# A two-layer graph network on one core: where the work buffers start in on-chip memory, modulo 64 bytes

## The chip, the core and the metric

The kernel runs on one core of a Trainium2 chip. The metric is the device time of one execution in microseconds. Before the change it is 2314.32 us, the median of three runs (2314.19 to 2317.76).

## What is computed

There are 128 graphs of 128 nodes with 256 features, `x[128,128,256]`, and an integer matrix `adj[128,128,128]`. Two layers follow each other for every graph, and no graph touches another. All is fp32.

Layer 0 (called A in the kernel):

```
q, k, v = x@Wq.T+bq, x@Wk.T+bk, x@Wv.T+bv          # 8 heads of 32
p = softmax(where(adj == 0, -16384, q k^T))
z = v;  4 times:  z = 0.9 * p z + 0.1 * v
x1 = layernorm(x + z) * gamma + beta
```

Layer 1 (called B, its feed-forward part C):

```
n = layernorm(x1)*g1+b1;  q, k, v = n@wq+bq, ...
p = softmax(q k^T / sqrt(32) + where(adj > 0, 0.1*adj*adj, -inf))
x2 = x1 + (p v)@wo + bo
out = x2 + gelu((layernorm(x2)*g2+b2)@w1 + b1) @ w2 + b2      # 256 -> 1024 -> 256
```

## The kernel before

Two graphs form a pair, and 64 pairs go through the kernel. The work on a pair is cut into some 80 small steps (a projection, a quarter of the softmax, one hop of `z`, ...). Their order is written out by hand in three lists: a head, one turn that repeats through the middle (each turn takes every step once, for pairs 0 to 5 turns back, so that up to six pairs are in work), and a tail. All engines walk through the same list, and each does its part of the steps; semaphores tie them together. PSUM is a ring of four banks (`ring_ps`) beside four more banks for the attention scores (`score_ps`).

TensorE does two sorts of matrix products:

- Products with weights run in the type float32r on operands that are split into a high and a low part, three matmuls for each product (high·high, high·low, low·high; `by_parts`, lines 374 to 378, and `down`, lines 507 to 517). Each has 256 moving columns and a stationary operand of 128 columns, which a weight load (LDWEIGHTS) of its own brings in. In the projections (`project`) and in `up` a work buffer moves (`inT_A`, `inT_B`, `inT_C`) and the weight is stationary. In `values`, `output` and `down` the weight moves and a work buffer is stationary (`inT_A`, `inT_B`, `oT`, `hT`).
- Scores, hops, and the transposes run on plain fp32. In a transposition the unit matrix `ident` moves and the work buffer is stationary; in scores and hops both operands are work buffers.

In the rows of the trace an operation is written out<-moving,stationary, and the digits at the end of buffer names are left out (`w_high` is `w1_high` on line 377 and `w2_high` on line 515).

The diff touches only the place of buffers in SBUF. `sb(name, shape)` (line 198) takes the next free bytes of every partition, in the order of the calls, and each buffer begins at a multiple of 32 bytes. Worked out from the shapes and this rule, the places are, as a remainder by 64 (by 128 in brackets):

| buffers | before | after |
|---|---|---|
| all weights of the float32r products (`wA`, `wB`, `wo`, `w1`, `w2`) | 0 (0) | 0 (0) |
| the bias, gamma and beta rows | 32 (32) | 32 (32) |
| `ident` | 32 (32) | 0 (64) |
| all work buffers from `x_sb` to `hT_low` | 0 (64) | 32 (32) |

Every slice that a matmul reads starts at a multiple of 512 bytes within its buffer (128 in the hops), so an operand has the remainder of its buffer. The order of the steps, the instructions, and the semaphores are not touched.

Of the kernel before, what the change touches and what calls it, by code (L numbers as in the profile page):

```python
# [13 lines left out]
P = 128  # L14
# [171 lines left out]
def build(nc, x, xT, adj, WqT, bq, WkT, bk, WvT, bv, gamma, beta, ln1_g, ln1_b, ln2_g, ln2_b,  # L186
# [10 lines left out]
    with ExitStack() as ctx:  # L197
        def sb(name, shape, dt=F32):
            return ctx.enter_context(nc.sbuf_tensor(name, shape, dt))
# [18 lines left out]
        bvA_row, bvB_row = sb("bvA_row", [P, H]), sb("bvB_row", [P, H])  # L218
        gamma_row, beta_row = sb("gamma_row", [P, H]), sb("beta_row", [P, H])
        bo_row, b2_row = sb("bo_row", [P, H]), sb("b2_row", [P, H])  # L220
        ident = sb("ident", [P, P])
        tenth, eps, minus_half = sb("tenth", [P, 1]), sb("eps", [P, 1]), sb("minus_half", [P, 1])


        sb("apart", [P, 16])
        x_sb = sb("x_sb", [P, GB, H])
        xT_sb = sb("xT_sb", [P, C, T])
        adj_sb = {l: sb(f"adj_{l}", [P, GB, P], I32) for l in "AB"}
# [702 lines left out]
```

## Time and profile before

| | us | share |
|---|---|---|
| median of three runs | 2314.32 | |
| the profiled execution | 2317.23 | |
| its span, first to last instruction | 2315.4 | |
| TensorE busy (PE) | 2266.6 | 98% |
| weight loads (PEld) | 2154.3 | 93% |
| ScalarE busy (ACT) | 1926.8 | 83% |
| VectorE busy (DVE) | 1749.9 | 76% |
| GpSimd busy (POOL) | 1520.4 | 66% |

PE's busy time is the union of its matmuls, which overlap each other: one of 276 ns may follow the one before it by 113. So the busy time tells that the engine always had work, not how fast it went; for that the start times in the order of time are to be read. Weight loads run beside the matmul before them.

### The profile page before, as it was taken

To read this page: it belongs to the slowest core of one execution; us is meant where nothing else is said; L and a number is where in the kernel's file an instruction comes from. 1 tells how busy PE (TensorE), PEld (TensorE's weight loads), DVE (VectorE), ACT (ScalarE), POOL (GpSimd) and SP (SyncE) were. 2 spreads that over 40 slices of the span, in tenths; PEclk is the share of its full clock that TensorE was granted. 3 is DMA by queue.
4 is the path that set the end of the run, shared out by engine and by line. 5 is a ranking of instruction groups with operands and counts; after the bars stand their busy time and mean duration, and the time that the engine had idled before them with its cause. 6 is when DMAs were issued, how large, how long until landed. Compare 5 with 4: busy or idle time off the path is not lost. (4 is left out here: it accounts for less than half of the span.)

```text
span 2315.4 us, 78263 instructions
## 1 busy us (share of the span) xinstructions
PE 2266.6 (98%) x29492; PEld 2154.3 (93%) x29492; DVE 1749.9 (76%) x6993; ACT 1926.8 (83%) x6478; POOL 1520.4 (66%) x1613
## 2 busy tenths in 40 slices
PE   5999999999999999999999999999999999999997
PEld 5899999999999999999999999999999999999987
DVE  3888777787787787787787787787787787778883
ACT  5788888898898898898898898898888888888874
POOL 4766666676666666667666666666666667676551
PEclk8999999999999999999999999999999999999998
DMA  4110101101101101101101101101101101101000
GB/s 124 32 29 22 39 25 34 38 25 34 39 25 34 38 23 36 38 20 39 39 20 38 38 20 39 38 21 38 39 20 39 38 20 38 38 21 43 16 15 15
DMA packets 95781, 76.88 MB, mean 33 GB/s; under 512 B 9648, under 2 KB 95152, under 8 KB 95408
## 3 DMA queue, kind: packets, MB, share of 16 engines
q1 hardware_dynamic: 94176, 71.73, 10.0%
q8 instruction: 239, 3.92, 0.7%
q14 instruction: 134, 1.10, 0.2%
q10 hardware_dynamic: 1232, 0.14, 0.0%
HBM read 55.06 MB, written 16.78 MB: 31 GB/s over the span
## 5 line engine op out<-in xcount | busy, mean ns | idle before, releaser
L580 ACT ACTIVATE probs<-probs,negmax 128x128 f32<-128x128 f32 x2048 | 797.0, 398 | 28.1 <-DVE negmax L704 22.0
L862 POOL TENSOR_TENSOR probs<-probs,rinv 128x512 f32<-128x512 f32 x512 | 534.3, 1064 | 138.7 <-DVE rinv L718 138.4
L580 ACT ACTIVATION_READ_ACCUMULATOR probs<-probs,negmax 128x1 f32 x2048 | 402.3, 196 | 0.0
L601 ACT ACTIVATE zT<-ring_ps 128x512 f32<-128x512 f32 x256 | 157.8, 617 | 182.4 <-PE ring_ps L459 182.2
L377 PE MATMUL ring_ps<-inT_C_high,w_high 128*128 128x256 f32 x1024 | 302.4, 295 | 5.3 <-DVE inT_C_low L675 4.0
L515 PE MATMUL ring_ps<-w_high,hT_high 128*128 128x256 f32 x1024 | 296.8, 290 | 1.0 <-DVE hT_low L790 1.0
L451 PE MATMUL ring_ps<-ident,probs 128*128 128x128 f32 x2048 | 293.3, 276 | 3.1 <-ACT hT_high L621 1.6
L515 PE MATMUL ring_ps<-w_low,hT_high 128*128 128x256 f32 x1024 | 286.5, 280 | 0.0
L515 PE MATMUL ring_ps<-w_high,hT_low 128*128 128x256 f32 x1024 | 286.2, 279 | 0.0
L377 PE MATMUL ring_ps<-inT_C_high,w_low 128*128 128x256 f32 x1024 | 285.8, 279 | 0.0
L377 PE MATMUL ring_ps<-inT_C_low,w_high 128*128 128x256 f32 x1024 | 285.8, 279 | 0.0
L790 DVE TENSOR_TENSOR hT_low<-hidden,hT_high 128x512 fp32r<-128x512 f32 x256 | 231.4, 905 | 62.5 <-ACT hT_high L621 56.2
L451 PEld LDWEIGHTS ring_ps<-ident,probs 128*128 128x128 f32 x2048 | 227.4, 141 | 29.5 <-issue 26.9
L704 DVE CUSTOM_DVE_ANT_0 probs<-score_ps,mask_B 128x128 f32<-128x128 f32 x1024 | 228.4, 283 | 29.2 <-PE score_ps L442 29.2
L868 POOL TENSOR_TENSOR rstd<-moments,eps 128x2 f32<-128x2 f32 x192 | 39.4, 205 | 313.3 <-DVE moments L773 312.9
L704 DVE CUSTOM_DVE_ANT_0 probs<-score_ps,mask_A 128x128 f32<-128x128 f32 x1024 | 229.5, 283 | 4.3 <-PE score_ps L442 3.1
L621 ACT ACTIVATE hidden<-ring_ps,b_col 128x256 f32<-128x256 f32 x512 | 218.8, 490 | 13.9 <-PE ring_ps L377 9.9
L621 ACT ACTIVATE hT_high<-ring_ps,b_col 128x256 fp32r<-128x256 f32 x512 | 220.9, 503 | 0.0
L459 PE MATMUL ring_ps<-probsT_A,z 128*32 128x128 f32 x6144 | 209.2, 277 | 1.2 <-DVE z L738 1.0
L757 DVE TENSOR_TENSOR x<-ring_ps,x1b 128x512 f32<-128x512 f32 x64 | 44.2, 690 | 209.9 <-PE ring_ps L377 203.6
L377 PEld LDWEIGHTS ring_ps<-inT_C_high,w_high 128*128 128x128 f32 x1024 | 194.7, 190 | 7.9 <-DVE inT_C_low L675 4.8
L377 PEld LDWEIGHTS ring_ps<-inT_C_low,w_high 128*128 128x128 f32 x1024 | 195.2, 191 | 0.0
(150 smaller groups left out, 7378.3 us busy)
## 6 DMA issues: line engine op xcount, KB each, us to landing
xT_sb<-in_xT_dram SPq DMA_DIRECT2D x64, 256.0 KB, 3.1
x_sb<-in_x_dram SPq DMA_DIRECT2D x64, 256.0 KB, 2.8
out_dram<-x SPq DMA_DIRECT2D x128, 128.0 KB, 1.9
adj_A<-in_adj_dram SPq DMA_DIRECT2D x64, 128.0 KB, 3.1
adj_B<-in_adj_dram SPq DMA_DIRECT2D x64, 128.0 KB, 2.3
probsT_B<-in_L_gnn_w_dram SPq DMA_DIRECT2D x1, 1024.0 KB, 7.8
qT_B<-in_L_gnn_Wq_dram SPq DMA_DIRECT2D x1, 256.0 KB, 3.6
kT_B<-in_L_gnn_Wk_dram SPq DMA_DIRECT2D x1, 256.0 KB, 4.8
```

The costliest lines, as they stand in the source:

```text
L377: mm = pe.matmul(dst, left(a, kc), right(b, kc), start=(n == 0), stop=(n == len(pairs) - 1))
L451: mm = pe.transpose(ring(name, g)[:, r * P:(r + 1) * P], probs[:, UNIT[l, b], half * HR + r, :], ident[:, :])
L459: mm = pe.matmul(ring(name, g)[r * HD:(r + 1) * HD, (b * C + c) * P:(b * C + c + 1) * P], src[:, b, h * HD:(h + 1) * HD], prT[:, b, h, :], ...
L515: mm = pe.matmul(ring(name, g)[:, 0:H], hT[a][:, f, b * P:(b + 1) * P], w2_p[c][:, f, :], start=(n == 0), stop=(n == len(pairs) - 1))
L580: e = act.activation(probs[:, u, h, :], probs[:, u, h, :], ACT.Exp, bias=negmax[:, u, h:h + 1], scale=-1.0, accum_out=sums[:, u, h:h + 1])
L601: act.activation(zT[k][:, :, :, :], ring(name, g).rearrange("p (b c n) -> p b c n", b=GB, c=C), ACT.Copy).then_inc(s_out[name], 1)
L621: e = act.activation(dst[:, i, :], ring(name, g)[:, i * T:(i + 1) * T], ACT.Gelu, bias=b1_col[:, 2 * f + i:2 * f + i + 1])
L704: t = dve.tensor_tensor_reduce(probs[:, u, h, :], score_ps[:, r, (b * C + half) * P:(b * C + half + 1) * P], mask[l][:, b, :], -1.0, HIGHE ...
L757: dve.tensor_tensor(x2[:, :, :], ring(name, g).rearrange("p (b n) -> p b n", b=GB), x1b[:, :, :], ALU.add).then_inc(s_out[name], 1)
L790: dve.tensor_tensor(hT[1][:, 2 * f:2 * f + 2, :], hidden[:, f % 2, :, :], hT[0][:, 2 * f:2 * f + 2, :], ALU.subtract).then_inc(s_h_low, 1)
L862: pool.tensor_tensor(probs[:, u, hs, :], probs[:, u, hs, :], rinv[:, u, hs].unsqueeze(2).to_broadcast([P, HR, P]), ALU.mult).then_inc(s_pr ...
L868: pool.tensor_tensor(rstd[n][:, :, :], moments[n][:, :, 1:2], eps[:, :].unsqueeze(1).to_broadcast([P, GB, 1]), ALU.add).then_inc(s_shifted ...
```

## The change

Before, an unused buffer of 64 bytes stands between the constants and the work buffers. After, an unused buffer of 32 bytes stands in front of `ident`. With it `ident` and the three small constants move up by 32 bytes, and everything from `x_sb` on moves down by 32.

```diff
         bo_row, b2_row = sb("bo_row", [P, H]), sb("b2_row", [P, H])
+
+        sb("apart", [P, 8])
         ident = sb("ident", [P, P])
         tenth, eps, minus_half = sb("tenth", [P, 1]), sb("eps", [P, 1]), sb("minus_half", [P, 1])
 
-
-        sb("apart", [P, 16])
         x_sb = sb("x_sb", [P, GB, H])
```

## Rows read from the trace of the kernel before

**Rows 1.** The page: the span, and the granted TensorE clock in 40 slices.
```profile
span 2315.4 us, 78263 instructions
PEclk8999999999999999999999999999999999999998
```
**Rows 2.** Busy time by stretches: start:end, length, then each engine's busy us, PEclk.
```profile
50.00:1000.00 950.00, 944.02 (x12408) 895.68 (x12397) 739.12 (x2963) 805.84 (x2718) 644.22 (x679) 0.99 0.10 31
1000.00:2000.00 1000.00, 1000.00 (x13174) 955.43 (x13172) 766.21 (x3130) 856.84 (x2895) 676.01 (x717) 1.00 0.11 33
2000.00:2200.00 200.00, 198.88 (x2640) 188.69 (x2639) 159.23 (x609) 171.91 (x577) 131.42 (x139) 1.00 0.09 29
...
29.00:31.00 2.00, 2.00 (x12) 2.00 (x11) 0.67 (x7) 1.36 (x8) 1.20 (x2) 0.50 0.65 197
```
**Rows 3.** TensorE's waits: who waited for whom, us in total, times, longest.
```profile
PE ring_ps L377 <- POOL inT_A_low L843: 19.6, 2, 12.0
PE ring_ps L402 <- DVE n L784: 7.7, 3, 4.5
```
**Rows 4.** Order of time, the projections of B's q and k; start us, length us.
```profile
1010.52 0.28 PE L377 MATMUL ring_ps<-inT_B_low,wB_q_high 128*128 128x256 f32 x1
...
1013.11 0.28 PE L377 MATMUL ring_ps<-inT_B_high,wB_k_low 128*128 128x256 f32 x1
```
**Rows 5.** Order of time, two groups of the up projection.
```profile
1026.97 0.28 PE L377 MATMUL ring_ps<-inT_C_high,w_low 128*128 128x256 f32 x1
...
1029.35 0.28 PE L377 MATMUL ring_ps<-inT_C_high,w_low 128*128 128x256 f32 x1
```
**Rows 6.** Order of time, B's values at two times: after up, and after transposes.
```profile
114.47 0.28 PE L377 MATMUL ring_ps<-wB_v_high,inT_B_high 128*128 128x256 f32 x1
...
115.71 0.28 PE L377 MATMUL ring_ps<-wB_v_high,inT_B_low 128*128 128x256 f32 x1
...
1022.02 0.28 PE L377 MATMUL ring_ps<-wB_v_low,inT_B_high 128*128 128x256 f32 x1
...
1023.20 0.28 PE L377 MATMUL ring_ps<-wB_v_high,inT_B_low 128*128 128x256 f32 x1
```
**Rows 7.** Order of time at the lower clock, A's q and k.
```profile
29.06 0.41 PE L377 MATMUL ring_ps<-inT_A_high,wA_q_low 128*128 128x256 f32 x1
...
32.90 0.41 PE L377 MATMUL ring_ps<-inT_A_high,wA_k_low 128*128 128x256 f32 x1
```
**Rows 8.** Lines 377 and 515, matmuls by operands: count, shortest/median/longest ns.
```profile
L377 PE MATMUL ring_ps<-inT_C_high,w_low x1024: 276/276/416, 113.3 to 2306.3; 128*128 128x256 f32 x171
L377 PE MATMUL ring_ps<-inT_A_high,wA_q_low x256: 276/281/415, 8.2 to 2148.6; 128*128 128x256 f32 x128
L377 PE MATMUL ring_ps<-inT_A_high,wA_k_low x256: 276/276/415, 10.7 to 2173.4; 128*128 128x256 f32 x128
L515 PE MATMUL ring_ps<-w_low,hT_high x1024: 276/280/283, 125.3 to 2312.5; 128*128 128x256 f32 x171
```
**Rows 9.** Order of time and line 451: eight transposes with `ident` moving; its weight loads.
```profile
1019.16 1.04 PE L451 MATMUL ring_ps<-ident,probs 128*128 128x128 f32 x8
...
L451 PEld LDWEIGHTS ring_ps<-ident,probs x2048: 137/140/145, 36.1 to 2282.4; 128*128 128x128 f32 x187
L451 PE MATMUL ring_ps<-ident,probs x2048: 270/273/333, 36.1 to 2282.5; 128*128 128x128 f32 x187
```
**Rows 10.** Groups of VectorE and GpSimd, of equal shape: busy us, mean ns, idle before.
```profile
L757 DVE TENSOR_TENSOR x<-ring_ps,x1b 128x512 f32<-128x512 f32 x64 | 44.2, 690 | 209.9 <-PE ring_ps L377 203.6 <-DMA out_dram<-x 6.3
L692 DVE TENSOR_TENSOR v_A<-ring_ps,bvA_row 128x512 f32<-128x512 f32 x64 | 43.3, 676 | 4.9 <-PE ring_ps L377 4.7
L855 POOL TENSOR_TENSOR xv<-x_sb,xv 128x512 f32<-128x512 f32 x64 | 82.7, 1292 | 8.2 <-DMA x_sb<-in_x_dram 3.3
L891 POOL TENSOR_TENSOR x1b<-x,bo_row 128x512 f32<-128x512 f32 x64 | 82.2, 1285 | 6.3 <-DVE x L757 1.9
```
**Rows 11.** DMA issues: KB each, median us from issue to landing.
```profile
x_sb<-in_x_dram SPq DMA_DIRECT2D x64, 256.0 KB, 2.8
out_dram<-x SPq DMA_DIRECT2D x128, 128.0 KB, 1.9
```

## The prediction

> **What bounds the kernel now.** I read the page first: a span of 2315.4 us at almost the full TensorE clock [rows 1]. Then the busy time by stretches: from 50 to 2200 us TensorE is busy 2142.9 of 2150 us, and between 1000 and 2000 us it is never free at all, while ScalarE has work for 857 us of 1000 and VectorE for 766 [rows 2]. The waits of TensorE come to some 45 us in 17 kinds, and since those 1000 us have none, all of them lie towards head and tail; the two largest make up 27 us [rows 3]. So the middle of the kernel is one unbroken stream of TensorE instructions, and its length is the number of matmuls times the distance from one start to the next. That distance is what an address could change, and only the order of time shows it.
>
> It has two values for the same instruction. B's q and k: from 1010.52 to 1013.11 there are 22 steps, 117.7 ns each [rows 4]. The up projection: from 1026.97 to 1029.35, 21 steps of 113.3 ns [rows 5]. B's values were at 112.7 ns (11 steps in 1.24 us) early on, right after an up projection, and at 118 ns (10 steps in 1.18 us) in the middle, after transposes [rows 6]. So the value hangs not on the address alone but also on how the stream was entered. The recorded length gives away which of the two a group mostly has: a median of 276 ns goes with 113, one of 279 to 281 with 118 [rows 8]. By it the up projection (3 x 1024 matmuls) and A's k (3 x 256) run at 113.3, in all 3840, and the other 7680 at about 117.7: q of A, q and k of B, both values, the output (3 x 256 each, 4608 in all) and the down projection (3 x 1024).
>
> What would the distance be with nothing in the way? At the lower clock (granted 0.50, that is 1.2 GHz [rows 2]) it is 3.84 us over 18 steps, 213.3 ns [rows 7], or 256 columns at one per cycle, nothing added. At 2.4 GHz the same columns are 106.7 ns. So 6.7 or 11 ns are added at the fast clock, and these vanish when the reads come half as fast. That looks like two reads that get into each other's way, the moving operand and the next weights. The transposes give a second floor: eight of them last 1.04 us, so (1.04 - 0.273) / 7 = 109.6 ns apart [rows 9].
>
> **The change, part by part.** Nothing is added or removed but the address. It moves three things.
>
> (a) The other engines and the DMAs. Work buffers now start halfway through 64 bytes. On VectorE an addition that reads a row buffer, which already stands there, takes 676 ns, and one with both operands on whole 64 bytes takes 690; on GpSimd 1285 against 1292 [rows 10]. I cost this at 0. No row shows a write to such a place by an engine; bounded by these rows it is -2% to +2% on engines that are free 14% of the time, which TensorE's stream hides. The loads land in 2.8 us, and stores in 1.9 [rows 11]; they are started a turn ahead, so even 10% on them hides, except for the last store: +0.2 us. If the cover of ScalarE went (857 of 1000 us), its slack would be 143 us per 1000, far over 2%.
>
> (b) The products on plain fp32. Scores and hops have both operands in work buffers, so their distance to each other stays. The transposes keep a half-chunk distance, only with the sides exchanged. I cost both at 0.
>
> (c) The 11520 float32r matmuls. They are the pairs whose two operands get a new distance: both on whole 64 bytes before, one of them 32 bytes off after. No row shows such a pair in float32r; it is bounded from both sides.
> Lower end: the added time goes down to the floor of the transposes, the only pairs of TensorE that already stand 32 bytes apart. 3840 x (113.3 - 109.6) + 7680 x (117.7 - 109.6) = 14.2 + 62.2 = 76.4 us.
> Upper end: a stream that starts halfway touches 17 pieces of 64 bytes in place of 16, and if each costs its share of 106.7 ns (6.7 ns), the 6144 matmuls with a moving work buffer lose 41.0 us, and the 5376 with a stationary one up to 35.8 more: 77 us.
> Between them lies what this kernel shows it can do without any new state: all groups run at 113.3. That is 7680 x (117.7 - 113.3) = 33.8 us. I take this value, since the same instruction with the same addresses is seen at both [rows 6], and reads that no longer begin on the same boundary have the less to collide with.
>
> The stream passes on what it gains where it is unbroken, 2150 of 2315 us and the most of the rest: I count 95%, 32 us. By its own time the profiled execution goes from 2317.2 to 2285 us; the median of the runs lies 2.9 us lower, so the forecast is 2282 us. After it the next limit is still TensorE: ScalarE's 857 us would stand in 985.
>
> The page "TensorE: Matmul & The Clock Gate" of the Trainium skill (section "Wait — 56ns, not 53.3ns?") puts the warm distance at N / 2.4 + 2.5 ns. For 256 columns that would be 109.2 ns, and the rows here have 113.3 and 117.7, so the trace does not agree for this stream; by that figure alone nothing could be gained or lost through an address. The same page says (section "Step-by-step: what each phase is for") that the engine reads moving and stationary operands through two independent ports and that loading weights takes nothing from the running matmul. By this rule an address changes nothing and the time stays; the added 6.7 and 11 ns of the rows, which go away at the lower clock, speak against it, but don't prove a collision. It is the rival "no effect" below.
>
> **The rivals.**
> 1. No effect. Each operand is read ahead into a buffer wide enough that where it starts does not matter, and the added time is an exchange between weight load and matmul. For it: transposes start `ident` at 32 modulo 64 now and have the smallest added time of all [rows 9]; the value changes with the entry [rows 6], not with the place. Against it: two values for one instruction need something that depends on fine timing. Time: 2314, within 0.2%.
> 2. Down to the floor: the collision is one of equal boundaries and vanishes. 0.95 x 76.4 = 73 us: 2241. For it: only pairs 32 bytes apart show no excess. Against: a transpose loads its weights in 140 ns and moves half the columns, so it has fewer reads to collide.
> 3. The other side, mild: the new distance holds the stream in the slower of its two rhythms. The up projection and A's k, at 113.3 now, go to 117.7 [rows 5, 8]: 3840 x 4.4 x 0.95 = 16 us, 2330. It decides from the point where more than some 2000 of the 3840 fall (4.4 ns x 2000 = 9 us).
> 4. The other side, strong: the 17th piece. The 6144 moving streams alone cost 0.95 x 41 = 39 us (2353), with the stationary ones 73 us (2387). Against: `ident` touches one piece more than it need and pays nothing, but at half the column rate.
>
> **How the numbers follow.** Chances: forecast 0.27, rival 2 0.15, rival 1 0.25, rival 3 0.13, rival 4 0.20. A measurement of this kernel tells about 0.2% (4.6 us) from no change. Faster is the forecast and rival 2, 0.42; same is 0.25; slower is rivals 3 and 4, 0.33. The range goes from 2240 (the whole floor) to 2335 (the mild loss with 5 us over it), which leaves out rival 4. The forecast's own range is 2270 to 2300, and it is the likeliest by little.
>
> **What would show it.** The start-to-start distance of B's q and k and of the down projection should read 113 in place of 118, and the medians of all groups on lines 377 and 515 should be 276 ns. If transposes and hops keep 109.6 ns and float32r goes to 109, it is rival 2. If all medians stand as they are, rival 1. Medians of 281 on the up projection: rival 3. A distance of 120 ns or more, a value that no group has now, and above all where a work buffer moves: rival 4. Were ScalarE's or GpSimd's means to change by over 2%, step (a) would be wrong. Were TensorE to wait in the middle turns, the stream would no longer be the bound, and the sum would not pass through.

## The result: 1.0% slower, and the profile after

| | before | after |
|---|---|---|
| median of four runs | 2315.19 us | 2339.59 us |
| span of the profiled execution | 2315.4 us | 2338.3 us |

The ratio is 1.0105 (95% interval 1.0089 to 1.0121): 24.4 us more, where I had forecast 32 us less. It lies outside the range of 2240 to 2335 us.

First the page of the kernel after: span, busy time by engine, and the granted clock in 40 slices.

```profile
span 2338.3 us, 78263 instructions
...
PE 2290.3 (98%) x29492; PEld 2177.8 (93%) x29492; DVE 1753.8 (75%) x6993; ACT 1930.9 (83%) x6478; POOL 1517.7 (65%) x1613
...
PEclk8999999999999999999999999999999999999998
```

The clock reads as in [rows 1]. VectorE, ScalarE and GpSimd are busy for 1753.8, 1930.9 and 1517.7 us, where it was 1749.9, 1926.8 and 1520.4. Only TensorE grew by more, by 23.7 us, about the difference of the spans (22.9). Next the busy time of the stretch from 1000 to 2000 us, and TensorE's largest wait:

```profile
1000.00:2000.00 1000.00, 1000.00 (x13023) 955.53 (x13022) 760.43 (x3087) 851.59 (x2854) 665.94 (x706) 1.00 0.10 32
```
```profile
PE ring_ps L377 <- POOL inT_A_low L843: 20.6, 2, 12.8
```

TensorE is still never free in these 1000 us, and the wait at the head is 1.0 us longer (it was 19.6 us [rows 3]). But the 1000 us hold 13023 matmuls in place of 13174 [rows 2], 1.15% fewer. That is the cost: each start comes later after the one before. The next rows are in the order of time of the kernel after (start us, length us): B's q and k, a group of B's values, and two groups of the up projection:

```profile
1018.93 0.28 PE L377 MATMUL ring_ps<-inT_B_low,wB_q_high 128*128 128x256 f32 x1
...
1021.57 0.28 PE L377 MATMUL ring_ps<-inT_B_high,wB_k_low 128*128 128x256 f32 x1
...
1030.66 0.28 PE L377 MATMUL ring_ps<-wB_v_high,inT_B_low 128*128 128x256 f32 x1
...
1031.74 0.28 PE L377 MATMUL ring_ps<-wB_v_high,inT_B_low 128*128 128x256 f32 x1
...
1035.56 0.28 PE L377 MATMUL ring_ps<-inT_C_high,w_low 128*128 128x256 f32 x1
...
1038.05 0.28 PE L377 MATMUL ring_ps<-inT_C_high,w_low 128*128 128x256 f32 x1
```

B's q and k: 2.64 us over 22 steps, 120.0 ns; it was 117.7 [rows 4]. B's values: 1.08 us over 9 steps, 120.0; it was 118 [rows 6]. The up projection: 2.49 us over 21 steps, 118.6; it was 113.3 [rows 5]. No family had a mean of 120 before. Single steps are no longer all alike, either: within one group of up they read 116, 123, 118, 121, 117, 125 ns. The medians of the lengths (shortest, median, longest) have all gone to 280 to 282, against 276 to 281 in [rows 8]; A's k, for one, from 276 to 282:

```profile
L377 PE MATMUL ring_ps<-inT_C_high,w_low x1024: 276/281/415, 110.8 to 2329.1; 128*128 128x256 f32 x171
...
L377 PE MATMUL ring_ps<-inT_A_high,wA_k_low x256: 277/282/415, 11.0 to 2195.7; 128*128 128x256 f32 x128
...
L515 PE MATMUL ring_ps<-w_low,hT_high x1024: 278/281/286, 122.9 to 2335.3; 128*128 128x256 f32 x171
```

All further step times of whole families are worked out in one way: the mean time between neighbouring starts of a group, from 300 to 2000 us of the trace, with a group's first two steps left out. The right measure of the addresses turned out to be their **distance**: the start of the moving operand less the start of the stationary one, modulo 256 bytes (experiments 4 and 6 to 9 show this). The first number of a heading is that of the families whose work buffer moves (q, k, up), the second that of those whose weight moves (values, output, down).

| family | before: 192 / 64 | after: 160 / 96 | us more in the trace |
|---|---|---|---|
| up | 113.4 | 118.7 | +12.9 |
| k of A | 113.3 | 119.4 | +1.4 |
| q of A | 117.8 | 117.1 | +0.2 |
| q, k of B | 117.8, 117.8 | 120.4, 120.0 | +1.8, +1.7 |
| down | 117.8 | 119.8 | +5.3 |
| values of A, of B | 117.8, 117.8 | 119.0, 119.7 | 0.0, +1.7 |
| output | 117.8 | 119.5 | +1.4 |
| transposes | 109.2 | 109.2 | all others: -1.3 |

The last column is taken over the whole trace, with all steps of up to 330 ns from start to start, and sums to 25.1 us. The longer ones, which are mostly waits in head and tail, take 2.5 us back, so that all steps together come to 22.6 us.

### The profile page after: what moved, and what is told of

It reads as the page before. It is cut to its first block and busy times, and to the rows that moved or that the text cites. A ratio compares the mean times of both kernels' runs of the same rounds, so it can differ in the third digit from the quotient of the medians.

```text
span 2338.3 us, 78263 instructions
## 1 busy us (share of the span) xinstructions
PE 2290.3 (98%) x29492; PEld 2177.8 (93%) x29492; DVE 1753.8 (75%) x6993; ACT 1930.9 (83%) x6478; POOL 1517.7 (65%) x1613
```

## The experiments

Each ran in five rounds beside the kernel before; the three that have TensorE alone ran once. The diffs are against the kernel before.

**1 to 3. Which part of the change does it?** `work_only` moves the work buffers and leaves `ident`:

```diff
-        sb("apart", [P, 16])
+        sb("apart", [P, 8])
```

> Work buffers at 32 modulo 64 as in the change, but the unit matrix stays at 32 too; weights at 0. Three theories of the 24 us that the change costs. PLACE (an operand that starts at 32 modulo 64 costs its own matmul or weight load time): 2339 +-3 us, and the transposes, whose two operands now both start there, lose some ns too. DISTANCE (what costs is that the two operands of one float32r matmul start 32 bytes apart modulo 64): 2339 +-3 us, all lines 377 and 515 at 119 to 120 ns from start to start, transposes as before. ENTRY (the unit matrix at 0 modulo 64 changes how a stream of float32r matmuls is entered after transposes): 2315 +-3 us.

Measured: 2338.61 us against 2316.18, ratio 1.0095 (1.0081 to 1.0109). Nearly the whole loss is in the move of the work buffers. Not every line went to 119 to 120 ns, as DISTANCE wanted: up is at 118.4 and down at 119.8, but B's q and k stay at 117.6 and 117.4, and A's k is at 117.4. Number 13 comes back to this.

`ident_only` moves `ident` and leaves the rest at its old place:

```diff
+        sb("before_ident", [P, 8])
         ident = sb("ident", [P, P])
...
-        sb("apart", [P, 16])
+        sb("apart", [P, 8])
```

> The unit matrix moves to 0 modulo 64 as in the change (32 unused bytes in front of it, 32 behind the constants), while the work buffers stay where they were before the change. PLACE and DISTANCE: 2315 +-3 us, float32r matmuls at 113.3 and 117.7 ns as before. ENTRY: 2339 +-4 us.

Measured: 2320.80 us, ratio 1.0019 (1.0010 to 1.0028). Transposes stay at 109.2 ns, and one family alone has moved: up, from 113.4 to 115.7 ns, 4.2 us by the trace. Up doesn't read `ident`; transposes run ahead of it. This one loss is of the kind of rival 3. The time lies between the two that were expected.

`no_apart` takes the unused buffer away, so that work buffers start at 0 modulo 128 and both distances are 128:

```diff
-        sb("apart", [P, 16])
```

> No unused buffer: work buffers at 0 modulo 128 like the weights (before: 64). PLACE and DISTANCE modulo 64: 2315 +-3 us, since modulo 64 nothing changes. DISTANCE modulo 128 (banks of 64 bytes in turn): it moves by over 5 us, most likely up, since both operands then begin on the same bank: 2325 to 2350 us.

Measured: 2336.36 us, ratio 1.0084 (1.0070 to 1.0098). All operands start on whole 64 bytes here, and the loss is nearly that of the change: up 119.0, B's q and k 120.1. So the loss needs no start halfway through 64 bytes.

**4. Place or distance?** `all_up_32` moves everything from the first weight on, by the 32 bytes by which the change moves a part:

```diff
+        sb("first", [P, 8])
         wA = {n: parts(f"wA_{n}", [P, C, H]) for n in "qkv"}
```

> Everything is moved up by 32 bytes, weights too: weights at 32 modulo 64, work buffers at 32 modulo 64 (96 modulo 128), so both operands of each float32r matmul start off a whole 64 bytes, while their distance is what it was before the change. PLACE: slower than the change, as both sides pay: 2339 to 2363 us. DISTANCE: 2315 +-3 us, with 113.3 and 117.7 ns.

Measured: 2315.45 us, ratio 0.9998 (0.9989 to 1.0007). The stretch from 1000 to 2000 us, then a group of the down projection and one of up:

```profile
1000.00:2000.00 1000.00, 1000.00 (x13197) 955.21 (x13196) 765.94 (x3129) 856.86 (x2902) 678.21 (x719) 1.00 0.11 33
```
```profile
1004.70 0.28 PE L516 MATMUL ring_ps<-w_high,hT_low 128*128 128x256 f32 x1
...
1007.17 0.28 PE L516 MATMUL ring_ps<-w_high,hT_low 128*128 128x256 f32 x1
...
1024.30 0.28 PE L378 MATMUL ring_ps<-inT_C_high,w_low 128*128 128x256 f32 x1
...
1026.68 0.28 PE L378 MATMUL ring_ps<-inT_C_high,w_low 128*128 128x256 f32 x1
```

21 steps each: 117.6 and 113.3 ns. Every family has its step time of before to 0.01 ns, though every operand of every float32r matmul now starts at 32 modulo 64. So a start at 32 modulo 64 costs an operand nothing by itself, and rival 4, the seventeenth piece, is refuted. What counts is the distance.

**5. Is it TensorE alone?** `micro` is no graph network: 30 float32r matmuls on end, each with its weight load, in groups with transposes between them, at many distances, all other engines idle:

```diff
+            for i in range(30): pe.matmul(*one(1024, 1024), start=True, stop=True)  # 0
+            turn()
+            for i in range(30): pe.matmul(*one(1088, 1024), start=True, stop=True)  # 64
```

> TensorE alone: no work of the network, only streams of 24 or 30 float32r matmuls (256 moving columns, a 128-column weight load each) from two buffers, every stream after four transposes (some after 16 small matmuls), with the moving operand's start varied against the stationary one's; the output is a copy of x. The other engines are idle. DISTANCE (TensorE's own two reads collide): the start-to-start time depends on the distance modulo 128 alone, 113 to 118 ns at 64, over 118 at 0 and 32, and it is the same when both operands are moved by 32, 64 or 96 bytes. OTHERS (the reads collide with those of ScalarE, VectorE or GpSimd, which use the same buffers in the kernel): all distances give the same time here, near 109 ns. With 128 columns the weight load should bind, with 512 the added time should be the same number of ns or less.

Below are the rows, 30 matmuls in each: distances 0 (L74), 32 (L78), 64 (L82), 96 (L86), then both operands moved up by 32, at distance 0 (L124), then 128 moving columns in place of 256, at 0 (L140) and 64 (L144). A row's length is a first step of about 0.20 us, 28 more, and 0.28 for the last. The windows row ahead of them shows that no other engine worked.

```profile
40.00:250.00 210.00, 210.00 (x1775) 203.27 (x1773) 0.00 (x0) 0.00 (x0) 0.00 (x0) 1.00 0.00 1
```
```profile
35.97 3.84 PE L74 MATMUL ps<-mov,sta 128*128 128x256 f32 x30
...
44.00 3.75 PE L78 MATMUL ps<-mov,sta 128*128 128x256 f32 x30
...
51.93 3.78 PE L82 MATMUL ps<-mov,sta 128*128 128x256 f32 x30
...
59.95 3.84 PE L86 MATMUL ps<-mov,sta 128*128 128x256 f32 x30
...
135.18 3.84 PE L124 MATMUL ps<-mov,sta 128*128 128x256 f32 x30
...
170.30 3.55 PE L140 MATMUL ps<-mov,sta 128*128 128x128 f32 x30
...
177.82 3.55 PE L144 MATMUL ps<-mov,sta 128*128 128x128 f32 x30
```

Distances 0 and 96: (3.84 - 0.20 - 0.28) / 28 = 120.0 ns; 32: 116.7; 64: 117.8. With both operands moved up together, L124 repeats L74 (and at 64 it is 117.75, as L82). The last 12 steps of each group, worked out from single starts, give 113.3 for a distance of 112 and of -64, and 120 for 128, 256, 512, 1024, 2048 and 4096 (-128, which is 128 modulo 256 too, gives 118.8). Distances that are 64 modulo 256 give two values: 113.3 at 320, 576 and 2112, and 117.8 at 64, 1088 and 4160. Groups in which three pairs of buffers take turns, as high and low parts do in the kernel, give the same as one pair: 120 at 0 and 96, 116.7 at 32, 117.8 at 64. The effect needs no other engine and no PSUM traffic but TensorE's own. With half the moving columns a step is still 111.7 ns at every distance, though the columns alone would take half of 106.7: something else sets the pace there, most likely the weight load (which no run separates), and the distance makes no difference.

**6 to 8. More distances in the kernel.** Each changes the size of `apart` alone: `[P, 24]` (`apart_96`, distances 224 / 32), `[P, 1040]` (`apart_4160`, further by 4096 bytes) and `[P, 528]` (`apart_2112`, by 2048):

> Unused buffer of 96 bytes in place of 64: work buffers at 96 modulo 128, weights at 0, unit matrix at 32. DISTANCE modulo 128: 96 is -32, a distance not yet seen; if only the size of the distance counts it is as 32 is, 2336 to 2342 us; if the order counts (which read comes first) it can be as good as 64 or better, 2300 to 2320 us.

> Unused buffer of 64 + 4096 bytes: distance 64 modulo 128 as before, but all distances between weights and work buffers grow by 4096. LOW BITS ONLY: 2315 +-3 us, and each step keeps its rhythm, 113.3 for A's k and the up projection, 117.8 for the rest. BIT OF 4096: A's q and k differ before in that bit alone, so they swap: q 113.3, k 117.8; time within 2300 to 2335.

> Unused buffer of 64 + 2048 bytes: distance 64 modulo 128 again, all distances grow by 2048. LOW BITS ONLY: 2315 +-3 us with the rhythms of before. If higher bits of the distance choose the rhythm (113.3 or 117.8), steps change sides and the time moves by up to 34 us down (all at 113.3) or 17 up.

Measured: `apart_96` 2326.32 us, ratio 1.0043 (1.0031 to 1.0056), between the two ranges that were expected. Up (224) is at 118.1, as -32 was for TensorE alone (118.3); down (32) is at 116.8, a little better than before, as 32 was there (116.7). `apart_4160` 1.0001 (0.9992 to 1.0009) and `apart_2112` 1.0003 (0.9994 to 1.0012), with all step times those of before. So 2048 or 4096 bytes more of distance don't count.

**9. Distances and entries, TensorE alone.** `micro_entries` repeats single distances from five different entries (an odd-sized matmul ahead of the transposes):

> TensorE alone again: streams of 24 float32r matmuls, for 14 distances of the moving operand's start behind the stationary one's (in bytes modulo 128), each with five entries: before the four transposes stands one matmul of 64, 74, 84, 94 or 104 columns, which shifts the moment at which the stream begins. The output is a copy of x. If the first stand-alone run read right: 64 has two steady rhythms, 113.3 and 117.8 ns, and the entry chooses; 0 is at 120 and 96 at 120 from every entry; 112 goes to 113.3 from every entry after some steps (there it was seen once). If the 113.3 at 112 was a chance of its entry, it will be 117 or more from some of them.

Measured, ns: 112 gives 113.3 from all five entries, 32 gives 116.7 from all, 88 and 96 give 120 (to 0.2). At 104 four of five entries give 130, steps of 122 and 138 in turn. The entries did not choose at 64: it gives 117.8 from all five, and -64 gives 113.3 from all three that it had. Two steady values at one distance are seen in `micro`, as said above, and in number 16; they are the two of [rows 6].

The run shows the period as well. In this order the rows are distance 112, 240, 1136, and 4208 (112 modulo 256) with three pairs of buffers in turn, 24 matmuls in each:

```profile
209.73 2.98 PE L176 MATMUL ps<-mov,sta 128*128 128x256 f32 x24
...
310.09 3.06 PE L236 MATMUL ps<-mov,sta 128*128 128x256 f32 x24
...
316.73 2.98 PE L240 MATMUL ps<-mov,sta 128*128 128x256 f32 x24
...
336.55 2.98 PE L252 MATMUL ps<-mov,sta 128*128 128x256 f32 x24
```

With 22 steps between the first and the last, 2.98 us is 113.6 ns and 3.06 us is 117.3. So 128 bytes more change the step, and 1024 or 4096 more don't: the distance counts modulo 256 and not modulo 128.

**10, 11. Distance 112 in the kernel.** Weights come out of buffers made larger than need be and cut so that they start elsewhere. The first cut, `threes_112`, left the distances a mix of 112 and 240; `all_112_of_256` mended that:

```diff
+        def placed(name, shape, at):
+            n = shape[1] * shape[2]
+            return tuple(sb(f"{name}_{part}", [P, n + 64], F32R)[:, at // 4:at // 4 + n].rearrange("p (c n) -> p c n", c=shape[1])
+                         for part in ("high", "low"))
+        STILL, MOVES = 16, 240
...
-        sb("apart", [P, 16])
```

> The kernel before with its weights moved so that in each float32r matmul the moving operand starts 112 bytes (modulo 128) behind the stationary one: work buffers at 0, weights that stay still (wA and wB of q and k, w1) at 16, weights that move (wA and wB of v, wo, w2) at 112. If 112 draws the stream to 113.3 ns in the kernel as it did by itself: all float32r groups at 113.3 but for the first steps, 34 us less than before at the most, 2285 to 2300 us. If the 113.3 was a chance, 2310 to 2340.

> In the run before, the parts of the weights lay 128 bytes apart in their remainder by 256, so that its distances were 112 modulo 128 but 112 and 240 in turn modulo 256; the stand-alone streams had 113.3 ns at 112 and 1136 and 117.3 at 240 and -16. Here every one of the 11520 float32r matmuls has its moving operand 112 bytes behind the stationary one modulo 256. PERIOD 256: all groups settle at 113.3 ns, after a first step of 209 or less; 7680 matmuls by 4.4 ns less than before, less some ns of settling in 640 groups: 2285 to 2298 us. PERIOD 128 (the stand-alone result was chance): 2332 us again.

Measured: 2332.02 us, ratio 1.0063 (1.0050 to 1.0077), and 2327.68, ratio 1.0044 (1.0030 to 1.0058). Both missed. In the second, down does settle at 113.3 ns after some 11 steps, but up alternates between 119 and 121 to its end, though its distance is the same. That three pairs of buffers take turns in the kernel is not the reason: row L252 above has them too and settles at 113.3. Part of the miss is the length of the groups. With TensorE alone 112 can need ten steps of 114 to 121 ns before it settles; down, 24 matmuls long, goes the same way, while the values and the output, 12 long, end where they would settle, with a mean of 117.7. Why up doesn't settle, though some of its groups are 24 long, stays open.

**12. A distance the kernel has shown to work.** `all_192_of_256` uses `placed` with STILL, MOVES = 0, 128 and leaves `apart` at 64 bytes: projections keep their 192, and the families whose weight moves get it too in place of 64.

> Work buffers where they were before the change; only the weights that move (v of both layers, wo, w2) are placed 128 bytes further, so that every float32r matmul has distance 192 modulo 256, where before the products with a moving weight had 64 and the others 192. In the stand-alone streams 192 was at 113.3 from four of five entries, 64 at 117.8 from seven of nine. PERIOD 256: values, output and down, 5376 matmuls at 117.8 before, go to 113.3 wherever their entry allows: 2291 us if all do, 2305 if half of them do. PERIOD 128: 2315 +-3 us.

(By the starts of both traces, one pair of buffers at a time, it was five of six groups at 113.3 for 192, and ten of thirteen at 117.8 for 64.)

Measured: **2299.78 us**, ratio 0.9926 (0.9912 to 0.9940): faster than both kernels. The stretch, a group of B's values, and one each of up and down:

```profile
1000.00:2000.00 1000.00, 1000.00 (x13331) 955.26 (x13329) 776.07 (x3161) 867.19 (x2927) 684.53 (x725) 1.00 0.11 33
```
```profile
1013.34 0.60 PE L408 MATMUL ring_ps<-ident,n 128*128 128x128 f32 x4
...
1014.02 0.28 PE L383 MATMUL ring_ps<-wB_v_high,inT_B_low 128*128 128x256 f32 x1
...
1015.04 0.28 PE L383 MATMUL ring_ps<-wB_v_high,inT_B_low 128*128 128x256 f32 x1
...
1018.82 0.28 PE L383 MATMUL ring_ps<-inT_C_high,w_low 128*128 128x256 f32 x1
...
1021.20 0.28 PE L383 MATMUL ring_ps<-inT_C_high,w_low 128*128 128x256 f32 x1
...
1028.76 0.28 PE L521 MATMUL ring_ps<-w_high,hT_low 128*128 128x256 f32 x1
...
1031.15 0.28 PE L521 MATMUL ring_ps<-w_high,hT_low 128*128 128x256 f32 x1
```

Values 113.3 (1.02 us over 9 steps), up 113.3, down 113.8; 13331 matmuls in the 1000 us, and TensorE is busy in all of them again. By the trace down gives 11.2 us, and the values and B's q and k 9.9 together. A's q and the output stay at 117.8 and 118.0.

**13, 14. The change cut in two by distance.** `half_project` gives 160 / 64 (STILL, MOVES = 0, 224, `apart` 32 bytes), `half_move` 192 / 96 (0, 32, `apart` 64 bytes).

> One half of the change: work buffers at 32 modulo 256, weights that stand still at 128, so projections and up have distance 160 as after the change; the weights that move go along by 32 bytes, so values, output and down keep their 64 of before. By the start times of the change's trace against those of before, up costs 12.9 us and q and k of both layers 5.1 us together: 2333 +-4 us. If the cost were in the start off a whole 64 bytes of each operand, values and down would pay too: 2339 or more.

> The other half: work buffers where they were before the change (distance 192 for projections and up), and only the weights that move are placed 32 bytes further, so that values, output and down have distance 96 as after the change. By the start times of the change's trace: down 5.3 us, values and output 3.1 us: 2325 +-4 us, and down at 119.8 ns.

Measured: 2325.07 us, ratio 1.0037 (1.0025 to 1.0050), and 2322.31, ratio 1.0024 (1.0014 to 1.0035). The rows, down and up of `half_project`, then of `half_move`, 21 steps each:

```profile
1004.02 0.28 PE L521 MATMUL ring_ps<-w_high,hT_low 128*128 128x256 f32 x1
...
1006.50 0.28 PE L521 MATMUL ring_ps<-w_high,hT_low 128*128 128x256 f32 x1
...
1028.98 0.28 PE L383 MATMUL ring_ps<-inT_C_high,w_low 128*128 128x256 f32 x1
...
1031.47 0.28 PE L383 MATMUL ring_ps<-inT_C_high,w_low 128*128 128x256 f32 x1
```
```profile
1002.05 0.28 PE L521 MATMUL ring_ps<-w_high,hT_low 128*128 128x256 f32 x1
...
1004.57 0.28 PE L521 MATMUL ring_ps<-w_high,hT_low 128*128 128x256 f32 x1
...
1027.01 0.28 PE L383 MATMUL ring_ps<-inT_C_high,w_low 128*128 128x256 f32 x1
...
1029.39 0.28 PE L383 MATMUL ring_ps<-inT_C_high,w_low 128*128 128x256 f32 x1
```

With 160 / 64 up is at 118.6 and down at 118.1 in these rows (118.1 and 117.8 over the whole family); with 192 / 96 up stays at 113.3 and down goes to 120.0 (family: 113.4 and 119.8). Each large family follows its own distance. The halves lose 8.5 and 5.7 us, together 14.2 of 24.4, and `half_project` missed its expectation by 8 us. By its trace that has three parts. Up loses 10.9 us in place of 12.9. A's values, whose distance is not touched, went from 117.8 to 113.3 (-3.2 us). And q and k of both layers lose 1.0 us in place of the expected 5.1. B's q and k of `half_project`:

```profile
1012.58 0.28 PE L383 MATMUL ring_ps<-inT_B_high,wB_q_low 128*128 128x256 f32 x1
...
1015.05 0.28 PE L383 MATMUL ring_ps<-inT_B_high,wB_k_low 128*128 128x256 f32 x1
```

That is 2.47 us over 21 steps, 117.6 ns (family: 117.6 and 117.4), at the distance of 160 at which the change has 120.4 and 120.0. `work_only`, with 160 too, has the same 117.6 and 117.4. Both leave `ident` at its old place, and the change moves it. So at 160 as well a family's step hangs on more than its distance, here by up to 3 ns.

In `half_move` q and k of B, not touched either, went from 117.8 to 115.4 and 113.3 (-1.5 and -2.8 us by the trace). A distance of 64 or 192 has two rhythms, and a family that sits in the slower one can fall into the fast one when something ahead of it changes. With the whole change no family has such a distance left.

**15. Does the entry choose?** `all_192_ident` is number 12 with `ident` up by 32 bytes, so every float32r distance stays 192:

> The kernel with all distances at 192 modulo 256 (2300 us), and the unit matrix moved up by 32 bytes to another distance from the work buffers. If the entry from the transposes chooses the rhythm, groups change sides: A's q and output may join the others at 113.3 ns (down by up to 5 us, 2295), or up and others drop to 117.8 (up by 5 to 15 us). If it does not matter: 2300 +-3 us with the same groups.

Measured: 2303.80 us, ratio 0.9945 (0.9932 to 0.9959), 4.0 us more than number 12 by the medians. B's values, after the same four transposes as above:

```profile
1013.58 0.28 PE L384 MATMUL ring_ps<-wB_v_high,inT_B_low 128*128 128x256 f32 x1
...
1014.64 0.28 PE L384 MATMUL ring_ps<-wB_v_high,inT_B_low 128*128 128x256 f32 x1
```

1.06 us over 9 steps is 117.8 ns, where number 12 has 113.3. The distance is the same and only the transposes ahead read `ident` from elsewhere. Up went from 113.5 to 115.7, as in `ident_only`.

**16. 160 by itself.** `micro_160b` repeats 160, 96, 192 and 64 with TensorE alone, from up to six entries and from several places:

> TensorE alone: streams of 30 float32r matmuls at distances 160, 96, 192 and 64 modulo 256, each from six entries (a matmul of 64, 70, 74, 80, 84 or 90 columns ahead of the four transposes), at two absolute places 128 bytes apart, and with 256 less or more. The output is a copy of x. DISTANCE MODULO 256: 96 at 120.0 always, 160 at 116.7 to 118, 192 at 113.3 and 64 at 117.8 from most entries, whatever the absolute place. If bits above 256 or the absolute place matter, rows of one distance differ by place rather than by entry.

Two rows each of 160, 96 and 192, in this order, 30 matmuls in each:

```profile
35.86 3.81 PE L74 MATMUL ps<-mov,sta 128*128 128x256 f32 x30
...
56.26 3.77 PE L84 MATMUL ps<-mov,sta 128*128 128x256 f32 x30
...
108.98 3.85 PE L110 MATMUL ps<-mov,sta 128*128 128x256 f32 x30
...
121.31 3.84 PE L116 MATMUL ps<-mov,sta 128*128 128x256 f32 x30
...
182.93 3.66 PE L146 MATMUL ps<-mov,sta 128*128 128x256 f32 x30
...
210.51 3.79 PE L160 MATMUL ps<-mov,sta 128*128 128x256 f32 x30
```

By the last 12 steps 96 gives 120.0 ns in 18 groups of 18; 160 gives 117.3 to 119.0, never 113.3. 192 gives 113.3 in 11 of 18 and 117.8 in 7, and 64 gives 113.3 in 4 and 117.8 in 14. The place of the pair may have a say in which: where the stationary operand starts at byte 2048 of its buffer, 192 is at 113.3 from all six entries and 64 from none, and with both operands 128 bytes further each is at 113.3 from three of six. The change swaps the two distances that can reach 113.3 for two that never did in these 36 groups.

## Why the prediction was wrong

**The bound** was right: TensorE's stream sets the time, the cost is in the time from start to start, and the other engines' busy times moved by some 4 us at most. What the stream lost came out in the end, as the prediction had it for a gain: 25 us by its steps without the waits, 22.9 in the span, 24.4 in the medians.

**Step (a)** held: VectorE's addition on line 757 still takes 690 ns [rows 10], and the loads and the last store land in 2.9 and 2.0 us, within 0.1 us of [rows 11].

```profile
L757 DVE TENSOR_TENSOR x<-ring_ps,x1b 128x512 f32<-128x512 f32 x64 | 44.2, 690 | 216.5 <-PE ring_ps L377 209.7
```
```profile
x_sb<-in_x_dram SPq DMA_DIRECT2D x64, 256.0 KB, 2.9
out_dram<-x SPq DMA_DIRECT2D x128, 128.0 KB, 2.0
```

**Step (b)** held for the transposes themselves (109.0 to 109.3 ns in all kernels). It missed what they do to the group behind them: `ident`'s move alone costs 0.2%, all of it in up.

**Step (c)** is the one that failed, and in its sign: "reads that no longer begin on the same boundary have the less to collide with" made it a gain of 33.8 us. That TensorE's two reads get into each other's way, as the prediction took from the added 6.7 and 11 ns, fits `micro`, where the time hangs on the distance of the two addresses with nothing else at work. But the old starts weren't on one and the same boundary in the sense that counts. They were 64 or 192 bytes apart of 256, and those are the only two multiples of 32 at which the fast rhythm was seen. With TensorE alone equal starts cost 120 ns and a distance of 128 cost 118.8 to 120. I had reduced everything to the remainder by 64, in which 0, 64, 128 and 192 look alike, while `no_apart` shows that between them lie 2336 and 2315 us. And I took the transposes as proof that 32 bytes apart is harmless; they move 128 columns, and with 128 columns float32r takes 111.7 ns at every distance. The text named that doubt under rival 2 and gave it too little weight. Sized by what was measured, the stream gets 25 us longer, where 33.8 less was worked out: up 12.9, down 5.3, the other families together 8.2, the rest -1.3. (Up's 5.3 ns x 3072 would be 16 us, but the first two steps of a group, 204 and 119 ns, did not grow.)

**Rival 1**, no effect, is refuted by the time and by micro; its remark that the transposes' added time is smallest while `ident` starts halfway was the same trap. **Rival 2** wanted 109 ns in float32r, which no kernel here had: the lowest steady value is 113.3. **Rival 3** (up and A's k from 113.3 to 117.7, +16 us) came nearest in size and place: those two families bear 14.3 of 25 us. It is right for `ident`'s part and is not the mechanism of the main part: at 96 and 160 none of 36 groups with TensorE alone showed the fast rhythm, and in the changed kernel all families but A's q (117.1) lie above the slow one, at 118.7 to 120.4. **Rival 4** had the sign and foresaw "a value that no group has now", 120 ns; its mechanism is refuted by `all_up_32`, and it had the size at 39 to 73 us. One reading of the prediction is off by its rounding: B's values early on are at 113.5 ns by the unrounded starts, not 112.7, so nothing in the kernel runs below 113.3 for long.

**The Trainium skill.** The page "TensorE: Matmul & The Clock Gate" says (section "Step-by-step: what each phase is for") that loading weights takes nothing from the running matmul, the two operands having ports of their own. These runs disagree for float32r: with all else idle, the distance between the two addresses makes a step of 256 columns last 113.3 to 120 ns, and 130 at one distance. Its N / 2.4 + 2.5 (section "Wait — 56ns, not 53.3ns?") gives an estimate of 109.2 ns for 256 columns, and no float32r group here reached it.

**What stays open.** The runs show the distance as the cause and TensorE as its place; how memory is divided so that 64, 112 and 192 can be fast and 0, 96, 128 and 160 can't, they don't show. Nor is it shown what in an entry picks the rhythm (in the kernel before, a first step of 206 ns mostly goes with 113.3 and one of 201 with 117.8, but B's values have 204 and 117.8), why B's q and k at 160 have 120 ns in the change and 117.5 in `work_only` and `half_project` (with TensorE alone 160 never went above 119.0), or why up doesn't settle at 112.

## What to carry to other kernels

Where a stream of float32r matmuls, each with a new stationary operand of 128 columns, is the bound, the distance between the start addresses of the two operands modulo 256 was worth 1.8% of this kernel (ratios 0.9926 and 1.0105 to the same kernel, with not one instruction changed): measure it, since here 64 and 192 were good, and 0, 96, 128 and 160 bad. A layout change far from a stream can move its rhythm too, by 0.2% here (`ident_only`). Look at the start-to-start distances, not at busy time, which is 98% in all of these kernels. Don't judge addresses by one remainder alone (64 here, where 256 counted), and don't take a floor from an instruction of another width, whose limit is another one.

## What the runs showed of the hardware that I had not expected

- The cost depends on the difference of the two addresses: 32 bytes more for both leave the kernel at 0.9998, 32 less for the work buffers alone make it 1.0095.
- The same stream at the same distance has two steady rhythms (113.3 and 117.8 ns at 64 and 192), and what runs ahead of a group, even where a transposition reads its unit matrix, can decide for the whole group (113.3 against 117.8 in B's values, numbers 12 and 15).
- At a distance of 104 bytes a step takes 130 ns from four of five entries, alternating between 122 and 138: 22% over the 106.7 ns of the columns alone.
- With 512 moving columns and TensorE alone a step takes 226.7 ns at distance 0, 228.9 at 64, and 233.3 at 32 and 96, against 213.3 for the columns: the order of the distances isn't the one of 256 columns.
